# Last attention layer: each head's memory matrix is folded into its output weights before the heads are read, and the features are scaled by a denominator spread over the partitions

## The chip, the cores and the metric

The kernel runs on one core of one Trainium2 chip. The metric is the device time of one execution in microseconds (us), the median of several runs. A core has TensorE (matmuls; PE in the rows below, its weight loads are PEld), VectorE (DVE), ScalarE (ACT), GpSimd (POOL) and SyncE (SP), which here issues most of the DMAs. Each runs its own list of instructions, and they wait for each other on semaphores.

## The reference

Four layers work one after the other on 1024 tokens of 512 channels. Each normalises its input, runs an attention and a feed-forward branch on it, and adds both. The change is in the attention of the last layer, a read from a fixed memory with 8 distinct heads of 128 channels. Only its output is returned; the updates of the memory are not computed by the kernel.

```python
q = (hidden_states @ Wq.T + bq).reshape(b, s, H, D)          # H = 32, D = 128
sig_q = jax.nn.elu(q) + 1.0
q_sel = sig_q[:, :, ::G, :]                                  # every 4th head: 8 are used
num = jnp.einsum('bshd,hde->bshe', q_sel, M)                 # M: [8, 128, 128]
den = jnp.einsum('bshd,hd->bsh', q_sel, z)[..., None] + EPS  # z: [8, 128]
retrieved = num / den
out_heads = jnp.repeat(retrieved, G, axis=2)
output = out_heads.reshape(b, s, H * D) @ Wo.T               # Wo: [512, 4096]
```

Because each of the 8 results is repeated four times, the four slices of `Wo` that belong to one head can be summed first. A head then adds (f M / (f z + eps)) Wsum to the output, where f is its features and Wsum is 128 x 512.

## The kernel before

The layers are stages that follow each other, with a barrier over four engines (`finish`) between the parts. Three stages matter here.

**The attention of the third layer** (about 810 to 1514 us). Groups of four query heads, 8 groups of 4 slots. Beside it, once per group, the kernel prepares Wsum of one head of the last layer. SP loads four slices into `wo3`, GpSimd adds them (`sum_wo`) into `G_wo`, ScalarE rounds the sum to the 32-bit "r" format for TensorE (`sum_head`, `WSH`), and GpSimd subtracts to get the rest (`WSL`). Every precise product of the kernel is done that way: operands are split into a rounded head (H) and a rest (L), and `product3` issues three matmuls (L x H, H x L, H x H).

**Normalisation and feed-forward of the last layer** (`normalise(3, ...)`, about 1516 to 1566 us). For each of 8 tiles of 128 tokens TensorE transposes the normalised tile, ScalarE copies it to `XNH`, and VectorE forms `XNL`. With a lag of two tiles TensorE runs the dense product (`unpacked_dense`, 12 matmuls of 512 columns), whose 4-bit weights are unpacked on VectorE, GpSimd and ScalarE first (`unpack_int4`, `W3H`, `W3L`). ScalarE and GpSimd also split the query weights (`L3H`, `L3L`).

**Reading the memory** (`recall`, about 1566 us to the end). 4 batches of 256 tokens by 8 heads make 32 steps. Head n passes through these on successive steps:

- TensorE: 12 matmuls of 256 columns give q (`qps`).
- VectorE: `G_m` = min(q + bias, 0). ScalarE: `G_e` = exp(G_m) and `G_r` = relu(q + bias). VectorE: `G_s` = G_e + G_r, the features, with channels on the partitions.
- TensorE, one step later: two full-precision matmuls (each appears in the trace as two passes, hence x4 in a row) with `G_s` as the stationary side and `MZ` (the memory matrix with z as a 129th column) as the moving side. Tokens are now on the partitions, numerator and denominator side by side.
- VectorE: adds eps to the 2 denominators of a partition, takes their reciprocal (`G_rec`, 128x2), and multiplies (`G_o`).
- TensorE: two transposes of `G_o`. ScalarE: `NH3`. VectorE: `NL3`. TensorE: `through_wo`, 6 matmuls of 512 columns with WSH and WSL, accumulated over the 8 heads.
- VectorE adds the result of a finished batch to `X`, and SP writes it out.

The order on each engine is that of the code, with `turns(n, lag)` telling which head's stage stands in step n. In the rows below L325 to L327 are the lines of `product3`, L578 is `copy` on ScalarE.

## Time and profile before

| | |
|---|---|
| median of 3 runs | 1689.52 us (1683.88 to 1691.61) |
| profiled execution, first to last instruction | 1693.6 us |
| that span against the median | 4.1 us longer |
| PE busy | 1574.8 us, 93% |
| DVE busy | 1127.2 us, 67% |
| ACT busy | 735.3 us, 43% |
| POOL busy | 431.8 us, 25% |
| mean granted TensorE clock | 0.949 of full speed |
| steps of `recall` from the first G_m to the last instruction | 1569.4 to 1693.6 us |

Busy time is the union of an engine's instructions. A matmul's shown duration overlaps the next one's, so the time that a matmul costs is read from start to start. In a row of the timeline a bracket gives how long the engine was idle before it and whose instruction ended that wait. The same holds on VectorE in a smaller way: two instructions that do not depend on each other start a little closer than one lasts.

### The profile page before, as it was taken

The numbers are of one execution on the slowest core, as the hardware profiler recorded it, in microseconds if no ns is written. First come the engines' busy times: TensorE is split into PE (matmuls) and PEld (weight loads), VectorE is DVE, ScalarE is ACT, GpSimd is POOL, SyncE is SP. The second block draws the span as 40 slices with busy tenths as digits, with TensorE's granted clock in tenths as the row PEclk, the third lists the DMA queues.
The fourth block names the chain that finished last, engine by engine and source line by source line (L and its number), as shares of the span: only waits on it lengthen the run. The fifth ranks groups of instructions, "written<-read, shape, count | busy, mean of one in ns | idle before, by whom it ended". The sixth has DMA issues, their size and how long they took to land.

```text
span 1693.6 us, 26835 instructions
## 1 busy us (share of the span) xinstructions
PE 1574.8 (93%) x9460; PEld 1309.7 (77%) x9460; DVE 1127.2 (67%) x2171; ACT 735.3 (43%) x1996; POOL 431.8 (25%) x328
## 2 busy tenths in 40 slices
PE   4999999998899997979999999999999999966998
PEld 3777776766577775757888888888888888955887
DVE  7555565656599997454677777777777677765454
ACT  3544454544222222132555555555555555532332
POOL 4000000001122217323332424242424343406000
PEclk9888899999899998959999999999999999987999
DMA  6000001001132300021020201011110102010000
GB/s 186 14 13 1 26 1 35 28 1 38 41 128 90 128 0 19 1 64 38 26 63 26 63 25 51 30 31 39 30 55 25 62 25 62 25 44 19 1 25 25
DMA packets 39683, 67.81 MB, mean 40 GB/s; under 512 B 4941, under 2 KB 13800, under 8 KB 39619
## 3 DMA queue, kind: packets, MB, share of 16 engines
q1 hardware_dynamic: 37522, 65.69, 12.3%
q10 hardware_dynamic: 2096, 1.30, 0.3%
q8 instruction: 37, 0.61, 0.1%
q14 instruction: 28, 0.22, 0.0%
HBM read 60.65 MB, written 2.13 MB: 37 GB/s over the span
## 4 chain that ended last, share of the span: by engine, by line
PE 70%; DVE 17%; issue 7%; POOL 3%; ACT 2%; DMA 1%; SPq 0%; POOLq 0%; DVEq 0%; ACTq 0%
PE PS L325 14%; PE PS L327 14%; PE PS L326 14%; PE PS L1525 5%; PE PS L1481 3%; DVE E_p L1253 3%; PE PS L1506 3%; PE PS L1527 3%; DVE E_nb L1244 2%; DVE E_mx L1240 2%; PE PS L1788 2%; PE PS L1459 2%; PE PS L1492 2%; DVE E_T L1262 1%; PE PS L1484 1%
## 5 line engine op out<-in xcount | busy, mean ns | idle before, releaser
L325 PE MATMUL PS<-XNH,E_WL 128*128 128x256 f32 x768 | 218.8, 285 | 6.7 <-POOL E_WL L440 5.9
L326 PE MATMUL PS<-XNL,E_WH 128*128 128x256 f32 x768 | 215.3, 280 | 0.0
L327 PE MATMUL PS<-XNH,E_WH 128*128 128x256 f32 x768 | 215.0, 280 | 0.0
L526 POOL TENSOR_TENSOR E_sw<-E_sw,rope2s 128x1024 f32<-128x1024 f32 x64 | 103.3, 1615 | 311.6 <-ACT E_sw L578 311.6
L1240 DVE TENSOR_REDUCE E_mx<-PS 128x4 f32<-128x512 f32 x64 | 60.8, 951 | 142.7 <-PE PS L1774 142.7
L325 PEld LDWEIGHTS PS<-XNH,E_WL 128*128 128x128 f32 x768 | 145.5, 189 | 11.1 <-POOL E_WL L440 8.9
L326 PEld LDWEIGHTS PS<-XNL,E_WH 128*128 128x128 f32 x768 | 145.2, 189 | 1.0
L327 PEld LDWEIGHTS PS<-XNH,E_WH 128*128 128x128 f32 x768 | 145.2, 189 | 0.0
L791 ACT ACTIVATE E_p<-PS,E_nb 128x128 f32<-128x128 f32 (+1 forms) x256 | 103.8, 431 | 86.7 <-DVE E_nb L1244 86.7
L578 ACT ACTIVATE E_sw<-PS 64x256 f32<-64x256 f32 (+1 forms) x128 | 89.5, 699 | 106.3 <-PE PS L327 104.8
L440 POOL TENSOR_TENSOR E_WL<-raw,E_WH 128x512 fp32r<-128x512 f32 x80 | 102.7, 1319 | 124.2 <-ACT E_WH L578 124.2
L1024 DVE TENSOR_REDUCE A_mx<-PS 128x4 f32<-128x512 f32 x64 | 61.3, 958 | 91.4 <-PE PS L1527 91.4
L457 POOL TENSOR_TENSOR A_sw<-A_sw,rope0s 128x256 f32<-128x256 f32 x32 | 23.3, 727 | 330.6 <-ACT A_sw L578 330.6
L325 PE MATMUL PS<-E_WH,OL 128*128 128x512 f32 x256 | 103.1, 403 | 1.4 <-DVE OL L1312 1.4
L1525 PE MATMUL PS<-kT,qT 64*128 64x256 f32 x256 | 100.5, 393 | 1.1 <-ACT kT L578 1.1
L327 PE MATMUL PS<-E_WH,OH 128*128 128x512 f32 x256 | 100.4, 392 | 0.0
L326 PE MATMUL PS<-E_WL,OH 128*128 128x512 f32 x256 | 100.0, 391 | 0.0
L1771 PE MATMUL PS<-QKH,QKL 128*128 128x256 f32 x256 | 91.5, 357 | 2.4 <-DVE OL L1312 2.4
L480 POOL TENSOR_TENSOR F_w<-F_t,scb 128x512 f32<-128x512 f32 x33 | 48.5, 1470 | 143.5 <-DVE F_t L973 143.5
L1253 DVE TENSOR_SCALAR E_p<-E_p,E_rec 128x128 f32<-128x128 f32 (+1 forms) x256 | 79.3, 373 | 2.3
L1409 PE MATMUL PS<-ident,ln_xn 128*128 128x128 f32 x128 | 29.3, 374 | 51.7 <-DVE ln_xn L920 51.7
L578 ACT ACTIVATE A_pT<-PS 128x512 f32<-128x512 f32 x32 | 19.1, 598 | 124.7 <-PE PS L1506 124.7
(266 smaller groups left out, 4602.7 us busy)
## 6 DMA issues: line engine op xcount, KB each, us to landing
raw<-in_w SPq DMA_DIRECT2D x104, 256.0 KB, 2.9
words<-in_words SPq DMA_DIRECT2D x11, 768.0 KB, 4.3
wo<-in_wo SPq DMA_DIRECT2D x32, 256.0 KB, 3.8
zb<-z_scratch SPq DMA_DIRECT2D x11, 384.0 KB, 4.9
scb<-in_scales SPq DMA_DIRECT2D x11, 384.0 KB, 5.5
X<-in_x SPq DMA_DIRECT2D x8, 256.0 KB, 5.1
SGH<-XNH SPq DMA_DIRECT2D x8, 256.0 KB, 2.7
SGL<-XNL SPq DMA_DIRECT2D x8, 256.0 KB, 2.8
```

Of the source, the lines that this page charges most:

```text
L325: nc.tensor.matmul(o, sl, mh, start=first, stop=False)
L326: nc.tensor.matmul(o, sh, ml, start=False, stop=False)
L327: return nc.tensor.matmul(o, sh, mh, start=False, stop=last)
L440: nc.gpsimd.tensor_tensor(lo, raw[:, slot, :], f32(hi), ALU.subtract).then_inc(w_lo, 1)
L526: nc.gpsimd.tensor_tensor(E_sw[:, heads, :], E_sw[:, heads, :], rope2s[:, :].unsqueeze(1).broadcast_to([P, heads.stop - heads.start, SEQ]) ...
L578: ins = nc.scalar.activation(o, i, ACT.Copy)
L791: last = nc.scalar.activation(E_p[:, blocks, :].rearrange("p n t -> p (n t)"), PS[:, 3 + 2 * tb + h // 2, at:at + (tb + 1) * P], ACT.Exp, ...
L1024: V.tensor_reduce(A_mx[:, 4 * tb:4 * tb + 4], PS[:, 2 * tb:2 * tb + 2, :].rearrange("p n (h s) -> p (n h) s", h=2)[:, :, 0:(tb + 1) * P], ...
L1240: V.tensor_reduce(E_mx[:, 4 * tb:4 * tb + 4], PS[:, 3 + 2 * tb:5 + 2 * tb, :].rearrange("p n (h s) -> p (n h) s", h=2)[:, :, 0:(tb + 1) * ...
L1253: last = V.tensor_scalar(E_p[:, blocks, :], E_p[:, blocks, :], E_rec[:, 4 * tb + h:4 * tb + h + 1], None, ALU.mult)
L1525: mm(PS[:, bank, at:at + SEQ], qT[r, n, tb * P:(tb + 1) * P], kT[r, n, :], start=True, stop=False, skip_group_check=True)
L1771: mm(o, QKL[:, h, t], QKH[:, 4, :], start=True, stop=False, skip_group_check=True)
```

## The change

The order of the products is changed from (f M) / den times Wsum to (f / den) times (M Wsum).

- The sums `WS` stay in full precision; `sum_head` on ScalarE and the subtraction on GpSimd are gone from the third layer's attention.
- In `normalise(3, ...)` TensorE computes M Wsum once per head (`fold`, one full-precision matmul of 512 columns, after the transposes of a tile). ScalarE rounds it to `MWH` (`fold_head`), VectorE forms `MWL` (`fold_rest`). 8 of each.
- A new input `zr3` holds z repeated over 128 columns (`ZR3`). With it as the stationary side and `G_s` as the moving side one matmul of 256 columns gives the denominator of all 256 tokens on every one of the 128 partitions. It replaces the product with `MZ`.
- VectorE adds eps to 128x256 denominators (`G_den`), takes the reciprocal of 128x256 (`G_rec`) and multiplies the features by it (`G_o`). Channels stay on the partitions, so the two transposes are gone, and `through_wo` comes a step earlier. `NH3` and `NL3` read `G_o` from SBUF and not the transposed copy in PSUM.

```diff
-            WSH = sb(late, "WSH", [P, H3, C], F32R)
-            WSL = sb(late, "WSL", [P, H3, C], F32R)
+            WS = sb(late, "WS", [P, H3, C])
...
-            MZ = sb(late, "MZ", [P, H3, P + 1])
+            MT3 = sb(late, "MT3", [P, H3, P])
+            ZR3 = sb(late, "ZR3", [P, H3, P])
+            MWH = sb(late, "MWH", [P, H3, C], F32R)
+            MWL = sb(late, "MWL", [P, H3, C], F32R)
...
-                G_rec = sb(st, "G_rec", [P, 2])
-                G_o = [sb(st, f"G_o{p}", [P, 2, P]) for p in range(2)]
+                G_den = sb(st, "G_den", [P, SEQ])
+                G_rec = sb(st, "G_rec", [P, SEQ])
+                G_o = [sb(st, f"G_o{p}", [P, SEQ]) for p in range(2)]
...
-            for t, name in [(bq3, "bq3"), (MZ, "mz3")]:
+            for t, name in [(MT3, "mt3"), (bq3, "bq3"), (ZR3, "zr3")]:
...
             def sum_wo(h):
 
                 pool.wait_ge(g3["woin"], h * 64 + 64)
-                after(pool, g3["wsl"], h)
                 nc.gpsimd.tensor_tensor(wo3[:, 0, :], wo3[:, 0, :], wo3[:, 1, :], ALU.add).then_inc(g3["s12"], 1)
                 nc.gpsimd.tensor_tensor(wo3[:, 2, :], wo3[:, 2, :], wo3[:, 3, :], ALU.add).then_inc(g3["s12"], 1)
                 pool.wait_ge(g3["s12"], h * 2 + 2)
-                nc.gpsimd.tensor_tensor(G_wo[:, :], wo3[:, 0, :], wo3[:, 2, :], ALU.add).then_inc(g3["s"], 1)
-                pool.wait_ge(g3["wsh"], h + 1)
-                at = bass.ds(h, 1)
-                nc.gpsimd.tensor_tensor(WSL[:, at, :].rearrange("p a n -> p (a n)"), G_wo[:, :],
-                                        f32(WSH[:, at, :]).rearrange("p a n -> p (a n)"), ALU.subtract).then_inc(g3["wsl"], 1)
+                nc.gpsimd.tensor_tensor(WS[:, bass.ds(h, 1), :].rearrange("p a n -> p (a n)"), wo3[:, 0, :], wo3[:, 2, :],
+                                        ALU.add).then_inc(g3["s"], 1)
...
-                def sum_head():
-                    act.wait_ge(g3["s"], g + 1)
-                    copy(WSH[:, bass.ds(g, 1), :].rearrange("p a n -> p (a n)"), G_wo[:, :], g3["wsh"])
...
+            def fold_head(h):
+                act.wait_ge(g3["mw"], h + 1)
+                copy(MWH[:, h, :], PS[:, 3 + 4 * (h % 2), :], g3["mwh"])
+
             def l3_heads(tt):
+                if tt >= 1:
+                    fold_head(tt - 1)
...
+            fold_head(H3 - 1)
...
-                    if turns(n, 2):
-                        act.wait_ge(g3["tp"], n - 1)
-                        after(act, g3["wo"], n - 3)
-                        copy(NH3[h % 2][:, :], PS[:, 4 + h % 2, 0:SEQ], g3["hi"])
+                    if turns(n, 1):
+                        act.wait_ge(g3["mul"], n)
+                        after(act, g3["wo"], n - 2)
+                        copy(NH3[1 - h % 2][:, :], G_o[1 - h % 2][:, :], g3["hi"])
...
-            normalise(3, between={1: unpack_int4, 3: int4_rests})
+            def fold_rest(h):
+                dve.wait_ge(g3["mwh"], h + 1)
+                V.tensor_tensor(MWL[:, h, :], PS[:, 3 + 4 * (h % 2), :], f32(MWH[:, h, :]), ALU.subtract).then_inc(g3["mwl"], 1)
+
+            def unpack_and_rest(tt):
+                if tt == 3:
+                    int4_rests()
+                fold_rest(tt - 3)
+
+            normalise(3, between={1: unpack_int4} | {tt: lambda tt=tt: unpack_and_rest(tt) for tt in range(3, 3 + H3)})
...
                         dve.wait_ge(g3["hi"], n - 1)
-                        V.tensor_tensor(NL3[h % 2][:, :], PS[:, 4 + h % 2, 0:SEQ], f32(NH3[h % 2][:, :]), ALU.subtract).then_inc(g3["lo"], 1)
+                        after(dve, g3["wo"], n - 3)
+                        V.tensor_tensor(NL3[h % 2][:, :], G_o[h % 2][:, :], f32(NH3[h % 2][:, :]), ALU.subtract).then_inc(g3["lo"], 1)
                     if turns(n, 0):
                         dve.wait_ge(g3["e"], n + 1)
                         dve.wait_ge(g3["r"], n + 1)
                         after(dve, g3["nps"], n - 1)
+                        after(dve, g3["mul"], n - 1)
                         V.tensor_tensor(G_s[h % 2][:, :], G_e[:, :], G_r[:, :], ALU.add).then_inc(g3["sum"], 1)
                     if turns(n, 1):
                         dve.wait_ge(g3["nps"], n)
-                        o = PS[:, 3 - h % 2, 0:2 * (P + 1)].rearrange("p (t e) -> p t e", t=2)
-                        V.tensor_scalar(G_rec[:, :], o[:, :, P], 1e-6, None, ALU.add).then_inc(g3["rc"], 1)
-                        dve.wait_ge(g3["rc"], n * 2 - 1)
-                        V.reciprocal(G_rec[:, :], G_rec[:, :]).then_inc(g3["rc"], 1)
-                        dve.wait_ge(g3["rc"], n * 2)
-                        after(dve, g3["tp"], n - 2)
-                        V.tensor_tensor(G_o[1 - h % 2][:, :, :], o[:, :, 0:P], G_rec[:, :].unsqueeze(2).broadcast_to([P, 2, P]), ALU.mult)\
-                         .then_inc(g3["mul"], 1)
-                    if h == 2 and turns(n, H3):
+                        after(dve, g3["rc"], n - 1)
+                        V.tensor_scalar(G_den[:, :], PS[:, 3 - h % 2, 0:SEQ], 1e-6, None, ALU.add).then_inc(g3["den"], 1)
+                        dve.wait_ge(g3["den"], n)
+                        after(dve, g3["mul"], n - 1)
+                        V.reciprocal(G_rec[:, :], G_den[:, :]).then_inc(g3["rc"], 1)
+                        dve.wait_ge(g3["rc"], n)
+                        V.tensor_tensor(G_o[1 - h % 2][:, :], G_s[1 - h % 2][:, :], G_rec[:, :], ALU.mult).then_inc(g3["mul"], 1)
+                    if h == 1 and turns(n, H3):
...
+            def fold(h):
+                if h == 0:
+                    pe.wait_ge(g3["in"], 16 * 3)
+                    pe.wait_ge(g3["s"], H3)
+                if h >= 2:
+                    pe.wait_ge(g3["mwl"], h - 1)
+                mm(PS[:, 3 + 4 * (h % 2), :], MT3[:, h, :], WS[:, h, :], start=True, stop=True).then_inc(g3["mw"], 1)
+
+            normalise(3, True, unpacked_dense, early=fold)
...
-                m = (h - 3) % H3
-                pe.wait_ge(g3["lo"], n - 2)
+                m = (h - 2) % H3
+                pe.wait_ge(g3["lo"], n - 1)
                 for tl in range(2):
                     t = slice(tl * P, (tl + 1) * P)
-                    last = product3(PS[:, 6 + tl, :], NH3[1 - h % 2][:, t], NL3[1 - h % 2][:, t], WSH[:, m, :], WSL[:, m, :],
+                    last = product3(PS[:, 6 + tl, :], NH3[h % 2][:, t], NL3[h % 2][:, t], MWH[:, m, :], MWL[:, m, :],
...
-                    if turns(n, 3) and h != 3:
-                        through_wo(n, h)
+                    if turns(n, 1):
+
+                        pe.wait_ge(g3["sum"], n)
+                        after(pe, g3["den"], n - 2)
+                        mm(PS[:, 3 - h % 2, 0:SEQ], ZR3[:, (h - 1) % H3, :], G_s[1 - h % 2][:, :], start=True, stop=True)\
+                            .then_inc(g3["nps"], 1)
                     if turns(n, 2):
-
-                        pe.wait_ge(g3["mul"], n - 1)
-                        after(pe, g3["lo"], n - 3)
-                        for tl in range(2):
-                            last = nc.tensor.transpose(PS[:, 4 + h % 2, tl * P:(tl + 1) * P], G_o[h % 2][:, tl, :], ident[:, :])
-                        last.then_inc(g3["tp"], 1)
-                    if turns(n, 1):
-
-                        pe.wait_ge(g3["sum"], n)
-                        after(pe, g3["mul"], n - 2)
-                        for tl in range(2):
-                            last = mm(PS[:, 3 - h % 2, tl * (P + 1):(tl + 1) * (P + 1)], G_s[1 - h % 2][:, tl * P:(tl + 1) * P],
-                                      MZ[:, (h - 1) % H3, :], start=True, stop=True, skip_group_check=True)
-                        last.then_inc(g3["nps"], 1)
-                    if turns(n, 3) and h == 3:
-                        after(pe, g3["xo"], b * 2)
+                        if h == 2:
+                            after(pe, g3["xo"], b * 2)
                         through_wo(n, h)
...
-        mz3=np.concatenate([a["L3_attn_M"], a["L3_attn_z"][:, :, None]], 2).transpose(1, 0, 2),
+        mt3=a["L3_attn_M"].transpose(2, 0, 1), zr3=np.broadcast_to(a["L3_attn_z"].T[:, :, None], (P, 8, P)),
```

VectorE, steps of `recall`, before. `PS` is the accumulator memory, `NL` is NL3; ISA and REGISTER_ALU are waits and address arithmetic.

```order
L1357 REGISTER_ALU
L1359 TENSOR_SCALAR G_m<-PS,bq 128x256
L1362 TENSOR_TENSOR NL<-PS,NH 128x256
L1367 TENSOR_TENSOR G_s<-G_e,G_r 128x256
L1371 TENSOR_SCALAR G_rec<-PS 128x2
L1372 ISA
L1373 RECIPROCAL G_rec<-G_rec 128x2
L1376 TENSOR_TENSOR G_o<-PS,G_rec 128x256
```

The same step on VectorE in the changed kernel.

```order
L1367 REGISTER_ALU
L1369 TENSOR_SCALAR G_m<-PS,bq 128x256
L1373 TENSOR_TENSOR NL<-G_o,NH 128x256
L1379 TENSOR_TENSOR G_s<-G_e,G_r 128x256
L1383 TENSOR_SCALAR G_den<-PS 128x256
L1386 RECIPROCAL G_rec<-G_den 128x256
L1388 TENSOR_TENSOR G_o<-G_s,G_rec 128x256
```

The places are the same six; the addition of eps and the reciprocal now work on 256 columns and not on 2.

TensorE, from the end of one head's query product to the start of the next, before. `WSH,NL` is the product with the output weights, `ident,G_o` the transposes, `MZ,G_s` numerator and denominator.

```order
L325 MATMUL PS<-XNH,L3L 128x256
L326 MATMUL PS<-XNL,L3H 128x256
L327 MATMUL PS<-XNH,L3H 128x256
L325 MATMUL PS<-WSH,NL 128x512
L326 MATMUL PS<-WSL,NH 128x512
L327 MATMUL PS<-WSH,NH 128x512
L325 MATMUL PS<-WSH,NL 128x512
L326 MATMUL PS<-WSL,NH 128x512
L327 MATMUL PS<-WSH,NH 128x512
L1859 MATMUL PS<-ident,G_o 128x128 x2
L1866 MATMUL PS<-MZ,G_s 128x129 x2
L325 MATMUL PS<-XNH,L3L 128x256
```

The same piece in the changed kernel.

```order
L327 MATMUL PS<-XNH,L3L 128x256
L328 MATMUL PS<-XNL,L3H 128x256
L329 MATMUL PS<-XNH,L3H 128x256
L1874 MATMUL PS<-G_s,ZR 128x256
L327 MATMUL PS<-MWH,NL 128x512
L328 MATMUL PS<-MWL,NH 128x512
L329 MATMUL PS<-MWH,NH 128x512
L327 MATMUL PS<-MWH,NL 128x512
L328 MATMUL PS<-MWL,NH 128x512
L329 MATMUL PS<-MWH,NH 128x512
L327 MATMUL PS<-XNH,L3L 128x256
L328 MATMUL PS<-XNL,L3H 128x256
```

The two transposes are gone, and the denominator's product stands ahead of the product with the output weights.

TensorE at the start of `normalise(3, ...)` in the changed kernel. Before, the first three tiles' transposes (12 of them) stood together, directly ahead of the first dense product.

```order
L329 MATMUL PS<-E_WH,OH 128x512
L1420 MATMUL PS<-ident,ln_xn 128x128 x8
L1840 MATMUL PS<-WS,MT 128x512
L1420 MATMUL PS<-ident,ln_xn 128x128 x4
L1840 MATMUL PS<-WS,MT 128x512
L327 MATMUL PS<-W3H,XNL 128x512
L328 MATMUL PS<-W3L,XNH 128x512
```

Two folds stand ahead of the first dense product; each of the other six stands between a tile's transposes (or, after the last transposes, a dense product) and the next dense product.

## Rows read from the trace of the kernel before

**Rows 1.** The page's head, and the granted TensorE clock in 40 slices.

```profile
span 1693.6 us, 26835 instructions
...
PEclk9888899999899998959999999999999999987999
```

**Rows 2.** Windows: stretch, its length, busy us of each engine, granted clock, DMA.

```profile
1500.00:1510.00 10.00, 7.32 (x35) 5.90 (x36) 6.77 (x13) 2.53 (x4) 0.00 (x0) 1.00 0.01 2
1600.00:1627.60 27.60, 27.15 (x186) 24.26 (x184) 15.18 (x47) 8.93 (x24) 0.00 (x0) 1.00 0.06 20
```

**Rows 3.** Timeline of VectorE and ScalarE, one step: start, us, engine, line, instruction.

```profile
1599.51 0.42 DVE L1367 TENSOR_TENSOR G_s<-G_e,G_r 128x256 f32<-128x256 f32 x1
...
1599.84 0.15 DVE L1371 TENSOR_SCALAR G_rec<-PS 128x2 f32<-128x2 f32 x1
...
1600.32 0.42 DVE L1376 TENSOR_TENSOR G_o<-PS,G_rec 128x256 f32<-128x256 f32 x1
...
1600.66 0.47 DVE L1359 TENSOR_SCALAR G_m<-PS,bq 128x256 f32<-128x256 f32 x1
...
1601.17 0.42 ACT L872 ACTIVATE G_e<-G_m 128x256 f32<-128x256 f32 x1 [2.03 <-DVE G_m L1359]
...
1601.49 0.46 ACT L873 ACTIVATE G_r<-PS,bq 128x256 f32<-128x256 f32 x1
...
1602.64 0.42 DVE L1362 TENSOR_TENSOR NL<-PS,NH 128x256 fp32r<-128x256 f32 x1 [1.51 <-ACT NH L578]
```

**Rows 4.** Timeline of VectorE: the additions to X at two batch ends.

```profile
1607.44 1.27 DVE L1382 TENSOR_TENSOR X<-X,PS 128x512 f32 x2
...
1636.18 1.27 DVE L1382 TENSOR_TENSOR X<-X,PS 128x512 f32 x2
```

**Rows 5.** Groups of VectorE by form: shapes, count, busy us, mean ns.

```profile
L1036 DVE RECIPROCAL A_rec<-A_sum 128x4 f32<-128x4 f32 x64 | 11.1, 173 | 6.7 <-ACT A_p L676 3.9 <-ACT raw L676 2.5
L1373 DVE RECIPROCAL G_rec<-G_rec 128x2 f32<-128x2 f32 x32 | 5.3, 166 | 1.1
L903 DVE RECIPROCAL ln_tmp<-ln_sd 128x8 f32<-128x8 f32 x4 | 0.8, 203 | 5.1 <-ACT ln_sd L592 5.1
...
L901 DVE TENSOR_SCALAR ln_var<-ln_mv 128x8 f32<-128x8 f32 x4 | 0.7, 172 | 0.1
```

**Rows 6.** Timeline of TensorE, one head of `recall` at full clock.

```profile
1674.03 0.38 PE L1859 MATMUL PS<-ident,G_o 128*128 128x128 f32 x2
...
1674.24 0.61 PE L1866 MATMUL PS<-MZ,G_s 128*128 128x129 f32 x4
...
1674.61 0.37 PE L325 MATMUL PS<-XNH,L3L 128*128 x1
...
1676.11 0.39 PE L325 MATMUL PS<-WSH,NL 128*128 128x512 f32 x1
...
1677.51 0.38 PE L1859 MATMUL PS<-ident,G_o 128*128 128x128 f32 x2
```

**Rows 7.** The last layer's normalisation: TensorE timeline, and a DMA issue with its landing.

```profile
1536.71 0.77 PE L325 MATMUL PS<-W3H,XNL 128*128 128x512 f32 x1 [5.52 <-DVE W3L L1345]
...
1541.97 0.71 PE L1409 MATMUL PS<-ident,ln_xn 128*128 128x128 f32 x4
...
MZ<-in_mz SPq DMA_DIRECT2D x1, 516.0 KB, 5.3
```

**Rows 8.** Timeline of GpSimd in the third layer's attention, once per group.

```profile
1116.41 1.29 POOL L553 TENSOR_TENSOR WSL<-G_wo,WSH 128x512 f32 x1 [3.64 <-ACT WSH L578]
1122.08 2.40 POOL L526 TENSOR_TENSOR E_sw<-E_sw,rope2s 128x1024 f32<-128x1024 f32 x1 [4.38 <-ACT E_sw L578]
```

**Rows 9.** Timeline of VectorE: first denominator, last product, last additions to X.

```profile
1574.25 0.15 DVE L1371 TENSOR_SCALAR G_rec<-PS 128x2 f32<-128x2 f32 x1
...
1685.36 0.42 DVE L1376 TENSOR_TENSOR G_o<-PS,G_rec 128x256 f32<-128x256 f32 x1
...
1689.63 1.28 DVE L1382 TENSOR_TENSOR X<-X,PS 128x512 f32<-128x512 f32 x2 [1.75 <-PE PS L327]
```

More of the change, by code:

```diff
@@ L209, in build_program @@
                 wo3 = sb(st, "wo3", [P, 4, C])
-                G_wo = sb(st, "G_wo", [P, C])
                 E_T = sb(st, "E_T", [P, 5, SEQ])
@@ L304, in build_program @@
         e2 = sems("e", "sc mx neg exp rec pn pt phi plo pv ohi olo pq pk sw vt t1 t2 q qhi qlo vtp vhi vlo wo x")
-        g3 = sems("g", "in woin s12 s wsh wsl qps m e r sum nps rc mul tp hi lo wo xo out")
+        g3 = sems("g", "in woin s12 s mw mwh mwl qps m e r sum nps den rc mul hi lo wo xo out")
         def turns(n, lag):
@@ L841, in l2_group @@
                     l2_slot(g, j, True, not first or j >= 1, not first or j >= 2, next_heads if j == NB - 1 and more else None,
-                            {1: wo_heads, 2: sum_head}.get(j))
+                            wo_heads if j == 1 else None)
             l2_group(0, True, True)
@@ L861, in _ @@
             normalise(3, each=l3_heads)
+            fold_head(H3 - 1)
             finish(act, 7)
-            act.wait_ge(g3["in"], 16 * 2)
+            act.wait_ge(g3["in"], 16 * 3)
             def recall(b, heads):
@@ L881, in _ @@
                 recall(b, range(H3))
-            recall(NB, range(3))
+            recall(NB, range(1))
             finish(act, 8)
@@ L1345, in int4_rests @@
                     V.tensor_tensor(W3L[:, k, :], t3[:, k, :], f32(W3H[:, k, :]), ALU.subtract).then_inc(f["lo"], 1)
-            normalise(3, between={1: unpack_int4, 3: int4_rests})
+            def fold_rest(h):
[6 more added lines that the diff above has]
+            normalise(3, between={1: unpack_int4} | {tt: lambda tt=tt: unpack_and_rest(tt) for tt in range(3, 3 + H3)})
             dve.wait_ge(bias_in, 3 * TT)
             finish(dve, 7)
-            dve.wait_ge(g3["in"], 16 * 2)
+            dve.wait_ge(g3["in"], 16 * 3)
             def recall(b, heads):
@@ L1386, in _ @@
                 recall(b, range(H3))
-            recall(NB, range(3))
+            recall(NB, range(2))
             finish(dve, 8)
@@ L1821, in unpacked_dense @@
                 dense_tile(3, tt, W3H, W3L)
-            normalise(3, True, unpacked_dense)
+            def fold(h):
[6 more added lines that the diff above has]
+            normalise(3, True, unpacked_dense, early=fold)
             finish(pe, 7)
-            pe.wait_ge(g3["in"], 16 * 2)
             pe.wait_ge(w_lo, U_L3 + H3)
-            pe.wait_ge(g3["wsl"], H3)
+            pe.wait_ge(g3["mwl"], H3)
             def through_wo(n, h):
-                m = (h - 3) % H3
-                pe.wait_ge(g3["lo"], n - 2)
+                m = (h - 2) % H3
+                pe.wait_ge(g3["lo"], n - 1)
                 for tl in range(2):
                     t = slice(tl * P, (tl + 1) * P)
-                    last = product3(PS[:, 6 + tl, :], NH3[1 - h % 2][:, t], NL3[1 - h % 2][:, t], WSH[:, m, :], WSL[:, m, :],
+                    last = product3(PS[:, 6 + tl, :], NH3[h % 2][:, t], NL3[h % 2][:, t], MWH[:, m, :], MWL[:, m, :],
                                     m == 0, m == H3 - 1)
@@ L1875, in _ @@
                 recall(b, range(H3))
-            recall(NB, range(3))
+            recall(NB, range(2))
             finish(pe, 8)
```

2 lines of the change are left out of this document (1 added, 1 removed).

## The prediction, made before the changed kernel was run

> **What bounds the kernel now.** I read the page first, then the windows of the last two stages, then the timeline of one step of `recall`, engine by engine. The page gives a span of 1693.6 us with the TensorE clock mostly near full [rows 1]. From 1600 to 1627.6 us TensorE is busy 27.15 of 27.60 us, VectorE 15.18, ScalarE 8.93 [rows 2]. So the reading of the memory is bound by TensorE, and the reader is to see in rows 3 how loosely VectorE hangs on it: `NL3` starts after 1.51 us of idle time. A head costs TensorE 3.48 us (transposes at 1674.03 and again at 1677.51): 0.21 for the two transposes, 0.37 for the four passes with MZ, 1.50 for the query product, 1.40 for the output weights [rows 6]. A whole batch of 8 heads takes 28.74 us (additions to X at 1607.44 and 1636.18), 3.59 a head [rows 4]. What matters is therefore whether the new step of VectorE fits in 3.5 us.
>
> **TensorE in `recall`.** The transposes go, 0.21 us a head. The denominator's matmul has two passes of 256 columns, 512 in all, against 4 x 129 = 516 before, so I keep 0.37. A head then costs 3.27 us. By that alone 32 heads save 7 us, but only while TensorE stays the bound.
>
> **VectorE in `recall`.** The two operations on 128x2 (0.15 and 0.17 us) become operations on 128x256. The addition of eps reads 256 columns of PSUM as G_m does: 0.47, with 0.03 to the next instruction 0.50. The product is 0.42 as before, and `NL3` 0.42 [rows 3].
>
> The reciprocal is the open price, since before no reciprocal is wider than 8. What there is: 166 ns at 2 columns, 173 at 4, 203 at 8, while another VectorE operation on 128x8 takes 172 [rows 5]. From 4 to 8 columns it grows by (203 - 173) / 4 = 7.5 ns a column; an ordinary operation on 256 columns takes 420 ns in all [rows 3], so under 2 ns a column. Carried on, 256 columns take 203 + 248 x 7.5 = 2063 ns. The lower end, if it were like an ordinary operation when wide, is 0.42 us. Between them, setting the extra time over the 128x8 operation (31 ns for 8 columns, 3.9 each) on top of 0.42 us gives 0.42 + 256 x 3.9 ns = 1.4 us. Upward, if the 166 ns at 2 columns hide a floor, the slope may be some 10% more: 2.3 us. I take 2.06, because the slope is a difference of two rows of the same operation and holds over 64 and 4 instances.
>
> The Trainium skill ("VectorE: DVE Perf Modes", First, the fixed hardware budget) says that the pipe runs Reciprocal as an iterative divide with a repeat count of 8. Read as 8 passes of one element each at the page's 0.96 GHz, my estimate from that page is 256 x 8 / 0.96 = 2.13 us and a fixed part, and the sum below would grow by some 5 us. Read as depth of a pipeline that still takes an element each cycle, it would be near 0.42 us. The slope of 7.5 ns speaks for the first reading; no row here shows a wide one.
>
> Now the step, by starts [rows 3]. From the product `G_o` to `G_m` 0.34 (1600.32 to 1600.66). G_m to G_e 0.51, G_e to G_r 0.32, G_r lasts 0.46, and with a handover of 0.05 `G_s` starts 1.34 after G_m. ScalarE's copy to `NH3` waits for `G_o` and runs beside G_m, about 0.05 + 0.42 us; `NL3` fits in the time in which VectorE waits for G_r. G_s to the addition of eps 0.33 (1599.51 to 1599.84), then 0.50, then the reciprocal 2.06 with 0.03 behind it. Sum: 0.34 + 1.34 + 0.33 + 0.50 + 2.09 = 4.60 us a step. TensorE needs 3.27 of these and is no longer the bound. Its order leaves room: the query product of the next head is queued behind this head's output product, which starts with `NL3`; that is 1.40 + 1.50 us later, before the 4.60 are over. VectorE is now late in everything: behind the reciprocal are queued G_o and the next G_m, for which ScalarE and then TensorE wait.
>
> Ends of `recall`. Before, the first denominator is handled at 1574.25, and the last G_o starts at 1685.36 [rows 9]. In the changed kernel the first G_o starts at 1574.25 + 0.50 + 2.09 = 1576.84; 31 steps of 4.60 and three pairs of additions to X, 1.2 each (a little under the 1.27 of a pair) [rows 4], put the last at 1576.84 + 142.6 + 3.6 = 1723.0. From the last G_o to the last additions to X it was 4.27 us [rows 9]; without a transposition and with `through_wo` a step nearer: G_o 0.42, NH3 0.42, NL3 0.42, three handovers 0.15, six matmuls and their end 1.6, so 3.0 us. The additions start at 1726.0 in place of 1689.63: +36.4 us.
>
> **The folds.** Each is two passes of 512 columns, 1024 in all, twice what the four passes with MZ stream: 2 x 0.37 = 0.74 us, or up to 2 x 0.58 = 1.16 if the transposes' time is counted to them [rows 6]. I take 0.9. Before the first dense product TensorE is idle for 5.52 us, waiting for `W3L` [rows 7]; the first two folds lie there. They wait for three DMAs: the last of before landed 5.3 us after its issue [rows 7], and one more of 512 KB comes behind it, still ahead of the third tile's transposes. `fold_head(0)` stands on ScalarE ahead of the copies to `W3H`, but the last of these is paced by GpSimd, so nothing moves. The other six folds lie between dense products, on the path: 6 x 0.9 = +5.4 us (4.4 to 7.0; 0 if hidden after all, 14 if all eight count at the lower clock). The 8 copies and 8 subtractions lie beside dense products of some 3 us each. If that cover were gone they would cost about 1 us per tile.
>
> **The third layer's attention.** ScalarE loses a copy and GpSimd a subtraction of 1.29 us per group. The subtraction came after 3.64 us of idle time and was followed by 4.38 us of idle time before the next instruction [rows 8]. Nobody waits for it, so it is worth 0. At most, 8 x 1.29 = 10 us, if GpSimd's place in the chain of waits were real.
>
> **Sum.** +36.4 + 5.4 = +41.8 us. The profiled execution's 1693.6 us become 1735.4; its span is 4.1 us over the median of 1689.5, so the median becomes 1731.
>
> **Rivals.**
>
> *Cheap reciprocal.* It costs 0.42 us when wide. VectorE's step is then 4.60 - 2.06 + 0.42 = 2.96 us, TensorE stays the bound with 3.27, and the change gives what it seems to promise: -0.21 x 32 = -6.7 us, -1.3 at the end, +5.4 for the folds, -2.6 in all: 1687. That is no change, and with the 10 us of GpSimd on top faster, 1677. It decides as soon as the reciprocal is under 2.06 - (4.60 - 3.27) = 0.73 us. For it: the fixed part of 166 ns dominates at 2 columns. Against: 7.5 ns a column in rows 5. 8%.
>
> *The clock falls as well.* TensorE would be busy 3.27 of 4.6 us, 71%, with a pause of some 1.3 us in each step. At the lower level (1.2 GHz) 12 matmuls of 512 columns take 5.26 us (1536.71 to 1541.97) [rows 7], 0.44 each, 0.22 for 256 columns: a head costs 2.6 + 2.6 + 0.8 = 6.0 us, 1.4 more than VectorE's step. Over all 32 steps that is +45, over half of them +22 on top: 1753. Against: from 1500 to 1510 us TensorE was busy 7.32 of 10 us with the clock at 1.00, its upper level of 2.4 GHz [rows 2]. 8%.
>
> *A reciprocal in between,* 1.4 us: the step is 3.94, the sum 31 x 0.66 = 20 us lower, 1711. 9%.
>
> **How the numbers follow.** Forecast 75%, cheap reciprocal 8%, clock 8%, in between 9%. The forecast's own range: reciprocal 1.8 to 2.3 us (-8, +7), folds 0 to 14 (-5, +9): 1718 to 1744. The range for 8 in 10 is 1710 to 1748. Half a per cent, 8.4 us, is about what a measurement of this kernel can tell from no change. Faster needs the cheap reciprocal and GpSimd's 10 us: 3%. Same 6%, slower 91%.
>
> **What would show it.** In the changed profile `G_rec` on 128x256 should last about 2.06 us, the additions to X should stand 8 x 4.6 + 1.2 = 38.0 us apart, VectorE should be busy over 85% of `recall` and TensorE some 70%, with a pause before the output product that ends with `NL3`. The dense tiles of the last layer should be 0.9 us further apart, and the third layer's groups as before. The forecast fails if `G_rec` is below 0.8 us, or if TensorE's clock reads near 0.5 in `recall`.

## The result: 2.0% slower

| | before | after |
|---|---|---|
| median | 1688.11 us (1683.88 to 1691.61, 4 runs) | 1721.19 us (1720.62 to 1723.43, 4 runs) |
| profiled span | 1693.6 us | 1718.8 us |
| mean granted clock | 0.949 | 0.954 |
| one batch of `recall`, additions to X to the next | 28.74 us | 35.90 us |
| first `ln_xn` of the last layer to the first G_m | 49.42 us | 51.25 us |

The ratio is 1.0203, with a 95% interval of 1.0181 to 1.0226. The forecast was 1731 us in a range of 1710 to 1748, so the time lies in the range, 10 us under the forecast.

The windows of the changed kernel, columns as in [rows 2], and the clock in 40 slices:

```profile
PEclk9898899999899998969999999999999999979999
```

```profile
1576.00:1578.00 2.00, 2.00 (x9) 1.72 (x7) 1.93 (x3) 0.00 (x0) 0.00 (x0) 0.50 0.04 8
1600.00:1627.60 27.60, 21.56 (x127) 17.60 (x127) 24.24 (x39) 6.99 (x18) 0.00 (x0) 1.00 0.06 20
```

In `recall` TensorE has dropped from 27.15 to 21.56 busy us of 27.60, VectorE has risen from 15.18 to 24.24, and the clock in that stretch is still full. Behind the first two query products it fell once in this trace, to 0.50 from about 1575.9 to 1578.9 us (the first window); TensorE had been idle for 2.67 us up to 1575.03. The step in which it fell took 5.70 us in place of 4.30, so 1.4 us of this trace are the clock's. This is one step on VectorE and ScalarE, the counterpart of [rows 3]:

```profile
1619.29 0.42 DVE L1388 TENSOR_TENSOR G_o<-G_s,G_rec 128x256 f32<-128x256 f32 x1
...
1619.63 0.48 DVE L1369 TENSOR_SCALAR G_m<-PS,bq 128x256 f32<-128x256 f32 x1
...
1619.75 0.42 ACT L576 ACTIVATE NH<-G_o 128x256 fp32r<-128x256 f32 x1 [3.13 <-DVE G_o L1388]
...
1620.14 0.42 ACT L873 ACTIVATE G_e<-G_m 128x256 f32<-128x256 f32 x1
...
1620.19 0.43 DVE L1373 TENSOR_TENSOR NL<-G_o,NH 128x256 fp32r<-128x256 f32 x1
...
1620.46 0.46 ACT L874 ACTIVATE G_r<-PS,bq 128x256 f32<-128x256 f32 x1
...
1621.01 0.42 DVE L1379 TENSOR_TENSOR G_s<-G_e,G_r 128x256 f32<-128x256 f32 x1 [0.39 <-ACT G_r L874]
...
1621.35 0.42 DVE L1383 TENSOR_SCALAR G_den<-PS 128x256 f32<-128x256 f32 x1
...
1621.80 1.75 DVE L1386 RECIPROCAL G_rec<-G_den 128x256 f32<-128x256 f32 x1
...
1623.59 0.43 DVE L1388 TENSOR_TENSOR G_o<-G_s,G_rec 128x256 f32<-128x256 f32 x1
```

From one G_o to the next it is 4.30 us, and every link stands in these rows: G_o to G_m 0.34, G_m to G_s 1.38 (with ScalarE's two functions between), G_s to G_den 0.34, G_den to the reciprocal 0.45, the reciprocal to G_o 1.79. The reciprocal's group by form is the one that answers to [rows 5]:

```profile
L1386 DVE RECIPROCAL G_rec<-G_den 128x256 f32<-128x256 f32 x32 | 56.1, 1753 | 1.1
```

TensorE's head, in answer to [rows 6]; the bracket says that it waits for VectorE's `NL3`:

```profile
1665.17 0.50 PE L327 MATMUL PS<-MWH,NL 128*128 128x512 f32 x1 [0.81 <-DVE NL L1373]
...
1668.07 0.59 PE L1874 MATMUL PS<-G_s,ZR 128*128 128x256 f32 x2
...
1669.48 0.50 PE L327 MATMUL PS<-MWH,NL 128*128 128x512 f32 x1 [0.81 <-DVE NL L1373]
```

The additions to X and the end, in answer to [rows 4, 9], on VectorE:

```profile
1609.82 1.28 DVE L1393 TENSOR_TENSOR X<-X,PS 128x512 f32 x2
...
1645.72 1.28 DVE L1393 TENSOR_TENSOR X<-X,PS 128x512 f32 x2
...
1711.75 0.42 DVE L1388 TENSOR_TENSOR G_o<-G_s,G_rec 128x256 f32<-128x256 f32 x1
...
1714.83 1.28 DVE L1393 TENSOR_TENSOR X<-X,PS 128x512 f32<-128x512 f32 x2 [1.75 <-PE PS L329]
```

The normalisation of the last layer, in answer to [rows 7], on TensorE:

```profile
1526.21 1.91 PE L1840 MATMUL PS<-WS,MT 128*128 128x512 f32 x2
...
1529.80 0.77 PE L327 MATMUL PS<-W3H,XNL 128*128 128x512 f32 x1 [1.68 <-DVE W3L L1346]
...
1534.95 0.63 PE L1420 MATMUL PS<-ident,ln_xn 128*128 128x128 f32 x4
...
1539.08 0.63 PE L1420 MATMUL PS<-ident,ln_xn 128*128 128x128 f32 x4
...
1539.55 1.02 PE L1840 MATMUL PS<-WS,MT 128*128 128x512 f32 x2
```

Tiles are 4.13 us apart and not 3.27, and the second fold lies in the idle time before the first dense product. Three parts make up the stage. From the first `ln_xn` to the first dense product it is 2.23 us shorter (14.49 and 16.72). From there to the last dense matmul it is 4.98 longer (32.02 and 27.04). The first query product, up to the first G_m, is 0.90 shorter (2.16 and 3.06), and that part is the clock: it was granted 0.77 there and 0.51 before.

The span is 25.2 us longer. Of these `recall`, from the first G_m (1566.56) to the end, is +28.05, and the normalisation +1.83. The rest is -4.65: the changed kernel reached its first `ln_xn` at 1515.31 and not 1519.99, and over all the traces here that point wanders from 1510 to 1529, also between kernels whose code up to there is the same. The two stages together are +29.9 us. The medians differ by 33.1, and by the interval of the ratio it is 31 to 38, so up to 3 us of the median's difference are not placed by the traces.

### The profile page after: what moved, and what is told of

The parts are those of the page before. It is cut to its first block and busy times, and to the rows that moved or that the text cites. A ratio compares the mean times of both kernels' runs of the same rounds, so it can differ in the third digit from the quotient of the medians.

```text
span 1718.8 us, 26625 instructions
## 1 busy us (share of the span) xinstructions
PE 1575.2 (92%) x9348; PEld 1295.4 (75%) x9348; DVE 1192.8 (69%) x2179; ACT 736.6 (43%) x1996; POOL 421.3 (25%) x320
## 3 DMA queue, kind: packets, MB, share of 16 engines
HBM read 61.17 MB, written 2.13 MB: 37 GB/s over the span
```

## The experiments

Ten kernels ran. Each comparison is with runs of the kernel before on the same chip. "After" is the changed kernel. Where two changed kernels are set against each other, their medians can come from different chips; the ratios give the same differences within 2 us.

### The division left out, one multiplication by 1 in its place (on after)

```diff
-                        V.reciprocal(G_rec[:, :], G_den[:, :]).then_inc(g3["rc"], 1)
+                        V.tensor_scalar(G_rec[:, :], G_den[:, :], 1.0, None, ALU.mult).then_inc(g3["rc"], 1)
```

> The changed kernel with the reciprocal of 128x256 replaced by a multiplication by 1 of the same 128x256 (the division is left out, everything else stays). Theory 'width': the reciprocal's 1.75 us alone makes VectorE the bound. The step of VectorE falls from 4.305 to about 4.305 - 1.79 + 0.33 = 2.85 us, below TensorE's 3.3, so TensorE is the bound again: batches 27 to 28 us apart in place of 35.9, time about 1721 - 4 x 8.3 = 1688. Rival 'chain': with the channels on the partitions the round trip VectorE, ScalarE, VectorE sets the step and the division is only a part; then the step stays at 3.7 us or more and the time above 1700.

Measured: 1696.81 us, ratio 1.0049 (1.0022 to 1.0077), batches 31.94 us apart. So 24 us of the 33 go with the division. But the step stops at 3.98 us, and TensorE, with 3.27 us of work, still waits. That is what the theory "chain" gave as its sign (3.7 us or more, over 1700 us), though the time is just under 1700; "width" had said 2.85 us of VectorE's time, so TensorE's 3.3, and 1688 us. The rows show the loop (TensorE and VectorE, not all rows):

```profile
1622.44 0.48 DVE L1369 TENSOR_SCALAR G_m<-PS,bq 128x256 f32<-128x256 f32 x1 [1.03 <-PE PS L329]
1622.84 0.41 DVE L1373 TENSOR_TENSOR NL<-G_o,NH 128x256 fp32r<-128x256 f32 x1
...
1623.31 0.50 PE L327 MATMUL PS<-MWH,NL 128*128 128x512 f32 x1 [0.48 <-DVE NL L1373]
...
1624.82 0.28 PE L327 MATMUL PS<-XNH,L3L 128*128 x1
...
1626.43 0.48 DVE L1369 TENSOR_SCALAR G_m<-PS,bq 128x256 f32<-128x256 f32 x1 [1.05 <-PE PS L329]
```

G_m waits for the query product, NL3 is queued behind G_m though its input is ready, the output weights' product waits for NL3, and the next query product is queued behind that: 0.40 + 0.47 + 1.51 + 1.61 = 3.99 us.

### The kernel before, with an unused reciprocal of 128x256 in each step

```diff
+                        after(dve, g3["xr"], n - 1)
+                        V.reciprocal(G_x[:, :], G_s[1 - h % 2][:, :]).then_inc(g3["xr"], 1)
                         dve.wait_ge(g3["rc"], n * 2)
```

> The kernel before with one more reciprocal of 128x256 on VectorE in each of the 32 steps, ahead of G_o; its result is used by nothing. Theory 'width': G_o comes 1.79 us later, and with it transposes, NH3 and NL3. Adding the links of the loop NL3, G_s, the two 128x2 operations, the new one, G_o, transposes, NH3: 0.34 + 0.33 + 0.19 + 0.20 + 1.79 + 0.47 + 0.49 + 0.42 = 4.2 us a step against 3.48, +23 us, about 1711. Rival 'cover': VectorE is idle for 1.51 us in each step and most of the new operation fits there: 3.48 + 0.28 = 3.8 us a step, +10 us, about 1698.

Measured: 1724.34 us, ratio 1.0201 (1.0173 to 1.0229), step 4.46 us, longer than either theory gave. This one instruction, in the kernel that has the transposes and none of the folds, costs as much as the whole change. VectorE and ScalarE in one step:

```profile
1586.85 1.73 DVE L1376 RECIPROCAL G_x<-G_s 128x256 f32<-128x256 f32 x1
1588.50 0.36 DVE L1379 TENSOR_TENSOR G_o<-PS,G_rec 128x256 f32<-128x256 f32 x1
1588.78 0.47 DVE L1360 TENSOR_SCALAR G_m<-PS,bq 128x256 f32<-128x256 f32 x1
...
1589.29 0.42 ACT L873 ACTIVATE G_e<-G_m 128x256 f32<-128x256 f32 x1 [3.41 <-DVE G_m L1360]
1589.61 0.46 ACT L874 ACTIVATE G_r<-PS,bq 128x256 f32<-128x256 f32 x1
1589.96 0.37 ACT L579 ACTIVATE NH<-PS 128x256 fp32r<-128x256 f32 x1
1590.37 0.42 DVE L1363 TENSOR_TENSOR NL<-PS,NH 128x256 fp32r<-128x256 f32 x1 [1.12 <-ACT NH L579]
```

VectorE is idle for 1.12 us in the same step, but not in that place: it waits for `NH3`, and on ScalarE that copy is queued behind the two functions that wait for G_m, which comes only after the reciprocal. The links are 0.28 + 0.51 + 0.32 + 0.35 + 0.41 from G_o to `NL3`, 0.94 from there to G_x (one step earlier in the trace), and 1.65 to the next G_o: 4.46 in all. The expectation had run its loop through the transposes and missed ScalarE's queue. After each of the three additions to X in the loop TensorE's clock fell to its lower level for 1.3 to 2.4 us (granted 0.54 from 1618 to 1620 us), and 0.5 to 0.6 us of each batch are owed to that.

### After, without the folds

`WSH`, `WSL` and their preparation as before; `through_wo` multiplies the scaled features by them, so that the product with M is left out.

```diff
-            normalise(3, True, unpacked_dense, early=fold)
+            normalise(3, True, unpacked_dense)
...
-  NL3[h % 2][:, t], MWH[:, m, :], MWL[:, m, :],
+  NL3[h % 2][:, t], WSH[:, m, :], WSL[:, m, :],
```

> The changed kernel without the folds: the output weights are split into WSH and WSL in the third layer's attention as before, and the features divided by the denominator go through them without the memory matrix (that product is left out). Theory 'folds and port': the six folds on TensorE's path cost 5.2 us, but they also moved GpSimd's L3L away from VectorE's W3L, which gave 2.1 back. Without them the stage from the first ln_xn to the first G_m takes 49.4 us again in place of 51.3, W3L's four subtractions 4.6 us in place of 2.5, and the time is about 1719. Rival 'attention': the 4.7 us by which the changed kernel reached the last layer earlier came from the work taken off ScalarE and GpSimd in the third layer's attention; then it is 3 us or more slower than the changed kernel, 1724 or more, and the groups of the attention are over 88.25 us apart.

Measured: 1718.41 us, ratio 1.0185 (1.0152 to 1.0217). By the medians the folds and all that goes with them cost 2.8 us, with intervals that overlap, so that isn't shown. The step stays at 4.305. `W3L` took 4.6 us again, as expected. The normalisation took 46.9 us and not 49.4: its first dense tile and its first query product were at the full clock sooner than in before (4.55 and 1.81 us, where before took 5.73 and 3.06). And the third layer's attention (first `E_mx` to first `ln_xn`) 703.57 us against 703.58 in after: taking the copy and the subtraction out of it gained nothing. (Before took 705.95 us there, but two other kernels with the same code in that stage took 703.41 and 703.63.)

### After, with the division as exp(-ln) on ScalarE

```diff
+            nc.scalar.add_instruction(mybir.InstLoadActFuncSet(..., act_func_set_id=6))   # once, ahead of recall
...
+                        nc.scalar.activation(G_den[:, :], PS[:, 3 - h % 2, 0:SEQ], ACT.Ln, bias=eps3[:, 0:1]).then_inc(g3["den"], 1)
...
+                        nc.scalar.activation(G_rec[:, :], G_den[:, :], ACT.Exp, scale=-1.0).then_inc(g3["rc"], 1)
...
-                        V.tensor_scalar(G_den[:, :], PS[:, 3 - h % 2, 0:SEQ], 1e-6, None, ALU.add).then_inc(g3["den"], 1)
...
-                        V.reciprocal(G_rec[:, :], G_den[:, :]).then_inc(g3["rc"], 1)
```

> The changed kernel with the reciprocal moved to ScalarE: logarithm of (denominator + eps) out of PSUM, then exp of its negative, both of 128x256, with one set of tables that holds both functions. VectorE loses the addition of eps and the reciprocal. Theory 'width': VectorE's step is about 2.1 us busy, ScalarE's five operations some 2.3, so TensorE bounds with about 3.3 us a step; batches 27.5 us apart, time 1721 - 33 = 1688 less 1 to 3 at the end: 1685 to 1689, about the kernel before. Rival 'chain': the loop through ScalarE, now with two more operations in it, sets the step: 3.8 us or more, over 1700.

Measured: 1701.99 us, ratio 1.0085 (1.0064 to 1.0106). The step is 3.98 us again, with VectorE busy 11.65 of 27.60 us: the same step as without the division, so neither the division nor ScalarE's two extra operations set it. The run with TensorE's order changed, below, tests that.

### After, both orders changed

TensorE's query product one head ahead (`project(n + 1)` before `through_wo` of step n), and on VectorE the denominator and the reciprocal ahead of G_s. The same instructions otherwise. (`zr` is the denominator's product.)

```diff
 VectorE: G_m(n)
-         NL3, G_s(n), G_den, G_rec, G_o
+         G_den, NL3, G_rec, G_s(n), G_o
 TensorE:
-         project(n), zr(n - 1), through_wo
+         zr(n - 1), project(n + 1), through_wo
```

> The changed kernel with the same instructions per head in another order: on TensorE the query product of the next head stands ahead of the output weights' product (one head ahead of before), on VectorE the denominator's addition and the long reciprocal stand ahead of the sum G_s. Theory (division's width): VectorE's own work per head is what it cannot go under: G_m, NL, G_s, G_den, G_rec and G_o take 0.34, 0.41, 0.34, 0.45, 1.79 and 0.34 us from start to start where nothing is waited for, 3.7 us, against a step of 4.305 us with its waits; so the step becomes 3.7 to 3.9 us, the batches 30 to 31 us apart instead of 35.90, the time 1700 to 1708 us. Rival (the chain minimum, exponential, sum, memory product, denominator, reciprocal, product is what lasts 4.3 us, whatever the order): the step stays within 0.1 us of 4.3 and the time at 1716 to 1725.

Measured: 1692.23 us, ratio 1.0029 (1.0005 to 1.0053): 29 us are back with every division still in place. The step, 3.49 us, and the time are under what was expected (3.7 to 3.9 us, 1700 to 1708). VectorE in one step:

```profile
1623.38 0.48 DVE L1369 TENSOR_SCALAR G_m<-PS,bq 128x256 f32<-128x256 f32 x1
1623.93 0.42 DVE L1373 TENSOR_SCALAR G_den<-PS 128x256 f32<-128x256 f32 x1
1624.27 0.41 DVE L1377 TENSOR_TENSOR NL<-G_o,NH 128x256 fp32r<-128x256 f32 x1
1624.60 1.75 DVE L1381 RECIPROCAL G_rec<-G_den 128x256 f32<-128x256 f32 x1
1626.27 0.36 DVE L1387 TENSOR_TENSOR G_s<-G_e,G_r 128x256 f32<-128x256 f32 x1
1626.54 0.41 DVE L1390 TENSOR_TENSOR G_o<-G_s,G_rec 128x256 f32<-128x256 f32 x1
```

The wait for ScalarE's G_r is gone, because the reciprocal now runs in it. An instruction that needs the one right before it also starts later: G_den to the reciprocal was 0.45 us, and G_den to NL3 is 0.34; the reciprocal to G_o was 1.79, and to G_s it is 1.67. VectorE is busy 26.93 of 27.60 us here. TensorE's 26.87 is nearly as much, but its work is 3.27 of the 3.49 us, so VectorE is the bound.

### Each order alone

```diff
 e10: VectorE's order as above, TensorE's as in after
 e11: TensorE's order as above, VectorE's as in after
```

> The changed kernel with VectorE's new order alone (denominator and long reciprocal ahead of the sum G_s); TensorE's order stays as in the changed kernel. Theory (two loops, each closed by another engine's order): VectorE alone could now go at 3.49 us a head, as it did with both orders, but the query product is still queued behind the output weights' product, which waits for NL, and NL now stands behind the denominator too: 0.31 from the end of the query product to G_m, 0.86 to the start of NL, 0.47 to the output weights' product, 1.5 for it and 1.3 for the next query product, 4.4 us a head. So the batches stay 35 to 36 us apart and the time at 1716 to 1725 us: half of the reordering gains nothing. Rival (the gain of 29 us came from VectorE's order): 3.5 to 3.7 us a head, 1693 to 1700 us.

> The changed kernel with TensorE's query product one head ahead alone; VectorE's order stays as in the changed kernel. Theory: the loop of the changed kernel runs over VectorE and ScalarE only (G_m, the exponential and the other half G_r on ScalarE, G_s, the denominator, the reciprocal, G_o and G_m again), so the step stays at 4.3 us, the batches at 35.9 less at most 1.2 us where the additions to X fall, and the time is 1716 to 1723 us. Rival (the gain came from TensorE's order): 3.5 to 3.7 us a head, 1693 to 1700 us.

Measured: 1715.88 us, ratio 1.0176 (1.0151 to 1.02), step 4.36 us with VectorE's order alone; 1719.38 us, ratio 1.0192 (1.0157 to 1.0226), step 4.305 with TensorE's alone. Both steps are as the two-loop theory says, and either rival (3.5 to 3.7 us, 1693 to 1700) is out. VectorE's row in the first, and in the second:

```profile
1625.01 0.48 DVE L1369 TENSOR_SCALAR G_m<-PS,bq 128x256 f32<-128x256 f32 x1 [0.91 <-PE PS L329]
```

```profile
1624.58 0.42 DVE L1379 TENSOR_TENSOR G_s<-G_e,G_r 128x256 f32<-128x256 f32 x1 [0.39 <-ACT G_r L874]
```

With TensorE's order alone the loop over VectorE and ScalarE is left, 4.30 us. With VectorE's order alone the loop over VectorE and TensorE is left, and it is longer than the 3.98 us that the run without the division showed: G_den now stands between G_m and `NL3`, 0.43 + 0.34 + 0.47 + 1.51 + 1.61 = 4.36. By the medians one order alone gains 5 us or 2, both with intervals that overlap the changed kernel's, so neither gain is shown; both together gain 29.

### Division on ScalarE and the query product ahead

The exp(-ln) kernel with TensorE's new order.

```diff
 TensorE:
-         project(n), zr(n - 1), through_wo
+         zr(n - 1), project(n + 1), through_wo
```

> The division as exp(-ln) on ScalarE, as in the run before it, and TensorE's query product one head ahead; nothing else differs. The step without the division on VectorE was 3.98 us in two kernels, though TensorE has 3.27 us of work per head. Theory (a loop over three queues): G_m 0.41, then NL 0.41 behind it on VectorE, the output weights' product that waits for NL 1.5, the next query product behind that on TensorE 1.4, and 0.3 until G_m of the next head: 3.98 us. With the query product ahead of the output weights' product the loop is open, the step becomes 3.3 to 3.5 us, the batches 26.5 to 28 us apart, the time 1683 to 1690 us, level with the kernel before or up to 0.4% under it. Rival (the chain through ScalarE's five operations sets 3.98): step within 0.1 of 3.98, time 1699 to 1705 us.

Measured: 1680.55 us (14 runs), ratio 0.9956 (0.9939 to 0.9972). This beats both kernels, the one before by 0.44%. The step of 3.98 us is gone, so the rival (ScalarE's five operations set it) is out. The windows and the additions to X:

```profile
1600.00:1627.60 27.60, 27.09 (x166) 24.15 (x166) 15.52 (x36) 17.32 (x43) 0.00 (x0) 1.00 0.06 20
```

```profile
1611.02 1.28 DVE L1397 TENSOR_TENSOR X<-X,PS 128x512 f32 x2 [1.56 <-PE PS L330]
...
1637.61 1.28 DVE L1397 TENSOR_TENSOR X<-X,PS 128x512 f32 x2 [1.55 <-PE PS L330]
```

A batch takes 26.59 us, 3.32 a head, and TensorE is the bound again. It is 28.74 - 26.59 = 2.15 us shorter than before; the transposes are 8 x 0.21 = 1.7 us of that by [rows 6]. The median is 21.4 us under the same kernel with the old order of TensorE, where 32 x (3.98 - 3.32) = 21.1 us were to be had. Two things keep this from showing that the change itself pays. The kernel before was not run with the query product ahead, so what that order alone gives isn't known. And the next experiment takes 4.6 us off the kernel before by a shift of some copies that the folds bring along as a side effect; against that kernel, 1683.21 us, 2.7 us are left, with intervals that overlap.

### The kernel before, with the copies of the query weights a tile later

```diff
-                if 2 <= tt < 6:
-                    for u in (2 * tt - 4, 2 * tt - 3):
+                if 3 <= tt < 7:
+                    for u in (2 * tt - 6, 2 * tt - 5):
```

> The kernel before, with ScalarE's copies of the query weights' high parts (L3H) one tile later in the norm stage, so that GpSimd's subtractions L3L fall behind VectorE's four W3L subtractions instead of beside them. Theory (the two engines hold each other up where both read two SBUF operands): the four W3L subtractions take 2.5 us instead of 4.6, and the norm stage (first ln_xn to first G_m) 47.3 us instead of 49.4. Rival (W3L was long for another reason, and the changed kernel's 2.5 us come from its dense tiles being later): W3L stays at 4.6 us and the stage at 49.4. Either way the time is within 3 us of 1689.

Measured: 1683.21 us, ratio 0.997 (0.9949 to 0.9992). VectorE's four subtractions in before, and in this kernel:

```profile
L1345 DVE TENSOR_TENSOR W3L<-t,W3H 128x512 fp32r<-128x512 f32 x4 | 4.6, 1211 | 0.0
```

```profile
L1345 DVE TENSOR_TENSOR W3L<-t,W3H 128x512 fp32r<-128x512 f32 x4 | 2.5, 676 | 0.0
```

So the two engines do hold each other up when they subtract at the same time. From the first `ln_xn` to the first dense product it is 16.6 to 16.7 us in four traces where L3L starts beside W3L (before, with the wide reciprocal, without folds, with the row of reciprocals) and 14.3 to 14.7 in the others. The whole stage took 45.8 us, 1.5 less than expected. Nearly all of that is the clock: from its start to the first G_m the first query product took 1.82 us here at a granted 1.00, and 3.06 us in before at 0.51. The same goes for the 2.4 us between before (32.70 us from the first dense product on) and the next kernel (30.30), whose code in this stage is the same: 1.15 us are the first dense tile (5.73 and 4.58) and 1.24 the first query product (3.06 and 1.82).

### Reciprocals of ten widths at the end of the kernel before

```diff
+            for width in (2, 8, 16, 32, 64, 128, 256, 512):
+                V.reciprocal(SW[:, at:at + width], G_src[:, 0:width])
```

> The kernel before with ten reciprocals after its last addition: 2, 8, 16, 32, 64, 128, 256 and 512 columns from SBUF, then 512 and 256 from PSUM. Theory: a fixed part of about 0.15 us and 6.25 ns for each column (six cycles of a 0.96 GHz clock), whatever the width: 64 columns 0.55 us, 128 columns 0.95, 256 columns 1.75, 512 columns 3.35, and the same from PSUM within 0.1 us. Rival: the price per column is not constant (7.5 ns at the narrow end, as between the widths of 8 and 16 in the norms, and less when wide): 64 columns over 0.60, 512 columns under 3.2 us. The ten take some 11 us at the end of the span.

Measured: 1698.54 us, one run. Groups by form, mean ns behind the busy time:

```profile
L1395 DVE RECIPROCAL SW<-PS 128x512 f32<-128x512 f32 x1 | 3.3, 3295 | 0.0
L1393 DVE RECIPROCAL SW<-XNH 128x512 f32<-128x512 f32 x1 | 3.3, 3294 | 0.0
L1393 DVE RECIPROCAL SW<-XNH 128x256 f32<-128x256 f32 x1 | 1.7, 1695 | 0.0
...
L1393 DVE RECIPROCAL SW<-XNH 128x128 f32<-128x128 f32 x1 | 0.9, 894 | 0.0
L1393 DVE RECIPROCAL SW<-XNH 128x64 f32<-128x64 f32 x1 | 0.5, 495 | 0.0
L1393 DVE RECIPROCAL SW<-XNH 128x32 f32<-128x32 f32 x1 | 0.3, 294 | 0.0
L1393 DVE RECIPROCAL SW<-XNH 128x16 f32<-128x16 f32 x1 | 0.2, 200 | 0.0
L1393 DVE RECIPROCAL SW<-XNH 128x8 f32<-128x8 f32 x1 | 0.2, 181 | 0.0
L1393 DVE RECIPROCAL SW<-XNH 128x2 f32<-128x2 f32 x1 | 0.2, 166 | 0.1
```

From 32 to 512 columns each doubling adds 6.2 to 6.3 ns a column, and 512 columns cost the same from PSUM as from SBUF. Below that the slope is another: 2.4 ns a column from 8 to 16. The theory of one price holds when wide and fails when narrow; the rival's steep narrow end is not there either.

## Why the prediction was right, and where it was off

- **VectorE becomes the bound of `recall`, and the wide reciprocal is why.** Right for this order of instructions. With the reciprocal's work out, 24 of 33 us go; put into the kernel before, it costs 35 us. But in a fitting order 29 of the 33 come back with every division in place, so it takes the long instruction and the order together. TensorE is seen waiting for `NL3`, and VectorE is busy 88% where over 85% was said. The clock rival fell: from 1580 to 1715 us the granted clock is 1.00, though TensorE is busy only 21.56 of 27.60 us (78%, where some 70% was said). Where the clock did fall, for 3 us near the start, that one step took 5.70 us.
- **The price of the reciprocal, 2.06 us.** Mis-sized: 1.75. It was carried on from 7.5 ns a column between 4 and 8 columns in [rows 5], rows of two different places in the program. The sweep shows that the narrow end has no such slope: its 166 to 200 ns are mostly a fixed part, and the true 6.25 ns a column appears from 32 on. That the guess came within 18% was luck: it is one reading of four that the same rows allowed, from 0.42 to 2.3 us. The Trainium skill ("VectorE: DVE Perf Modes", First, the fixed hardware budget) names an iterative divide with a repeat count of 8; read as 8 cycles a column that gave an estimate of 2.13 us. A price per column far above an ordinary operation's fits an iterative divide. But at the page's 0.96 GHz 6.25 ns is 6 cycles and not 8; the measurement decides.
- **The step of 4.60 us.** Right link by link: G_o to G_m 0.34 as said, G_m to G_s 1.38 for 1.34, G_s to G_den 0.34 for 0.33, G_den 0.45 for 0.50. Only the reciprocal's 1.79 for 2.09 counts. Over 31 steps the 0.295 us make 9.1 us. A batch was 35.90 for 38.0 us, and the end, G_o to the additions, 3.08 for 3.0. The forecast was +41.8 us and the two stages measured +29.9: 9.1 of the 11.9 between them are the reciprocal's price, 3.6 are the normalisation's, and the rest of `recall` came out 0.8 longer than forecast, with the clock's 1.4 in it.
- **The folds, +5.4 us.** The price was right (0.87 us a tile for 0.9, and the first two hidden), the step "so nothing moves" was wrong. `fold_head` delayed ScalarE's copies to `L3H`, so GpSimd's L3L fell behind VectorE's W3L. W3L went from 4.62 to 2.48 us, and the first dense product came 2.2 us sooner (14.49 us after the first `ln_xn`, not 16.72). The experiment on the kernel before makes the same 2.2 us (14.43) by itself. So +4.98 for the folds, -2.23 for that and -0.90 for the clock of the first query product give the stage's +1.83, but for rounding. The 2.2 us are luck and not the change's merit.
- **The third layer's attention, 0.** Right. In both kernels the `E_mx` stand three times 21.8 and once 22.9 us apart, 88.2 to 88.3 for four.
- **The cheap reciprocal's rival, 1687 us.** Its condition never held, but its price was wrong too: with 0.29 us in the reciprocal's place the kernel takes 1697. It was said that the query product queued behind the output weights' product would be ready before the 4.60 were over; that was true, and for this rival it was forgotten. The loop is 3.98 us long and lies above the 3.27 of TensorE's work.
- **What was not seen.** The sum held VectorE's wait for ScalarE, but took the order as given. The 4.30 us are not VectorE's work but a chain that leaves it waiting 0.39 us and starts each dependent instruction late. The same work in another order takes 3.49. So the change is slower because a long instruction stands in an order made for short ones. With the order that fits it the whole change leaves the kernel 0.3% slower (ratio 1.0005 to 1.0053).

## What to carry to other kernels

Before a tiny operation is made wide to save a transposition, its price per column has to come from a wide instance of the same operation; a slope between two narrow ones is noise on a fixed part. Then each loop that closes over the engines' queues has to be written down with its length, since the longest of them, and not the busiest engine, sets the step. Here a loop of 4.30 us hid one of 3.98, the order that opens the first lengthens the second to 4.36, and only both reorderings together gained. Where a product of weights is folded ahead, look at what its small copies push aside, for better or worse.
